# A transformer block on one core: where the biases of the projection are added, and on which engines its parts run

## The chip, the cores and the metric

The kernel runs on one core of a Trainium2 chip. The metric is the device time of one execution in microseconds (us); the time before is 3327.92 us, the median of 3 runs (3326.01 to 3333.78). One further execution was taken by the hardware profiler, and the rows below are from that one.

The core has five engines that run their own instruction lists and meet at semaphores: PE multiplies matrices and writes to PSUM, DVE and ACT and POOL work element by element, SP issues transfers.

## The reference

Four sequences of 1024 rows with 576 channels pass a block whose shifts, scales and gates come from a condition vector, and then a small rotation. What matters here:

```python
ada = silu(c) @ W_ada + b_ada
shift_msa, scale_msa, gate_msa, shift_mlp, scale_mlp, gate_mlp = split(ada, 6)
h = layernorm(x) * (1 + scale_msa) + shift_msa
x = x + gate_msa * (softmax_attention(h) @ W_proj + b_proj)
h = layernorm(x) * (1 + scale_mlp) + shift_mlp
x = x + gate_mlp * (gelu(h @ W_fc1 + b_fc1) @ W_fc2 + b_fc2)
x = rotate(x)
```

All of it is float32. A product of two float32 matrices is made of three products of rounded parts: each matrix is split into a high part (rounded) and a low part (what is left), and high x high, low x high and high x low are summed in PSUM. This is why there are so many instructions that make low parts.

## The kernel before

Six stages run one after another: preparation (ada, and the rotation matrices), the q, k, v products, attention, projection, feed-forward, rotation. A stage ends with a meeting of all engines.

**Preparation** also stores, beside the six parts of ada, two products: gate_msa x b_proj (GB_PROJ) and gate_mlp x b_fc2 (GB_FC2). So each bias can be added behind its gate.

**Attention** goes through 64 heads. SP loads each head's q, k, v three heads ahead (`load`), and sends the row maxima, which POOL has split, to the tiles that PE multiplies (`put_max`, L702). PE works through its list in order: the scores of a head cannot begin before its maxima have landed.

**Projection** works on 8 groups of 512 rows, in four subtiles t of 128 rows, and five channel tiles c of 128 (the last has 64). For a group g:
- *operand c*: PE spreads the reciprocal sums to 128 rows (`spread`, L1246), DVE multiplies the attention output with them (`operand`, L1105, tile p_of), ACT makes the high part (`operand_hi`, L1212), DVE the low part (`operand_lo`, L1110); both stand in p_oh.
- *product t*: PE multiplies p_oh with the weights p_w (`project`, L1258), 14 matmuls for each half of 288 columns, once all five operands of the group are there. DVE multiplies the result by the gate (`gate`, L1121) and adds the input rows (`residual`, L1126), to which POOL has added GB_PROJ (`biased_x`, L1059). The sum is p_x2.
- *statistics*: DVE's mean and variance (L1141 to L1158); then POOL normalises p_x2 into p_xn (L1071) and afterwards adds GB_FC2 to p_x2 (L1077), which SP stores for the next stage (L1017).
- *turn c*: PE transposes p_xn (L1285), ACT scales and shifts the result into the high part p_ht (L1232), DVE does the same in full precision into p_hf (L1191), POOL makes the low part (L1083), SP stores both (L1026).

The groups are interleaved by an order written out by hand, which every engine follows in its list. In the round of group g:

```python
ORDER = (("product", 0), ("product", 1), ("operand", 0), ("product", 2), ("operand", 1), ("turn", 0),
         ("turn", 1), ("product", 3), ("operand", 2), ("turn", 2), ("operand", 3), ("turn", 3),
         ("operand", 4), ("turn", 4))
```

Here "product" is of group g+1, "operand" of group g+2 and "turn" of group g. The statistics of group g come first in the round.

## Time and profile before

| what | us |
|---|---|
| median of 3 runs | 3327.92 |
| profiled execution | 3319.47 |
| its span | 3317.8 |
| attention's first and last matmul start | 727.16 and 1919.21 |
| projection's first product and last low part | 1948.12 and 2211.88 |
| feed-forward's first matmul | 2230.84 |
| PE, DVE, ACT, POOL busy over the span | 2939.1, 1698.6, 1400.5, 1525.1 |

An engine's busy time is summed over instructions that compute; issuing a transfer doesn't count. Matmuls overlap in the pipeline, so a row that merges 28 of them gives the time from the first start to the last end. In brackets stands the idle time of the engine before the row, and what ended it.

### The profile page before, as it was taken

To read this page: it belongs to the slowest core of one execution; us is meant where nothing else is said; L and a number is where in the kernel's file an instruction comes from. 1 tells how busy PE (TensorE), PEld (TensorE's weight loads), DVE (VectorE), ACT (ScalarE), POOL (GpSimd) and SP (SyncE) were. 2 spreads that over 40 slices of the span, in tenths; PEclk is the share of its full clock that TensorE was granted. 3 is DMA by queue.
4 is the path that set the end of the run, shared out by engine and by line. 5 is a ranking of instruction groups with operands and counts; after the bars stand their busy time and mean duration, and the time that the engine had idled before them with its cause. 6 is when DMAs were issued, how large, how long until landed. Compare 5 with 4: busy or idle time off the path is not lost. (4 is left out here: it accounts for less than half of the span.)

```text
span 3317.8 us, 49285 instructions
## 1 busy us (share of the span) xinstructions
PE 2939.1 (89%) x16066; PEld 2386.0 (72%) x16066; DVE 1698.6 (51%) x2862; ACT 1400.5 (42%) x1758; POOL 1525.1 (46%) x1143
## 2 busy tenths in 40 slices
PE   6759899968999999999999966849999999999976
PEld 2248777745666666666666645739999999999975
DVE  3446566546887888788887758741111111111125
ACT  2122222216888888888888822211111111111112
POOL 1232222115888878888888848752222222222210
PEclk9769899978999999999999978869999999999988
DMA  5365565552333333333333245658111121121144
GB/s 179 122 234 201 188 217 203 201 150 48 78 68 81 70 76 79 67 80 71 74 80 67 52 161 206 244 201 263 35 54 49 35 69 35 37 67 35 49 141 140
DMA packets 351132, 373.72 MB, mean 113 GB/s; under 512 B 179985, under 2 KB 243097, under 8 KB 350990
## 3 DMA queue, kind: packets, MB, share of 16 engines
q1 hardware_dynamic: 343512, 359.12, 36.4%
q10 hardware_dynamic: 7482, 12.69, 1.3%
q8 instruction: 95, 1.56, 0.2%
q14 instruction: 43, 0.35, 0.0%
HBM read 221.81 MB, written 149.36 MB: 112 GB/s over the span
## 5 line engine op out<-in xcount | busy, mean ns | idle before, releaser
L752 POOL TENSOR_TENSOR a_pl<-a_pf,a_ph 128x1024 fp32r<-128x1024 f32 x384 | 913.4, 2398 | 73.3 <-ACT a_pf L823 73.3
L769 DVE TENSOR_REDUCE a_mx<-a_psum_s 128x1 f32<-128x1024 f32 x512 | 625.9, 1222 | 246.4 <-PE a_psum_s L838 246.4
L821 ACT ACTIVATE a_ph<-a_psum_t 128x1024 fp32r<-128x1024 f32 x512 | 525.8, 1027 | 195.3 <-PE a_psum_t L853 195.0
L1407 POOL TENSOR_TENSOR m_al<-m_af,m_ah 128x256 fp32r<-128x256 f32 x288 | 212.1, 737 | 764.6 <-DVE m_ah L1416 764.6
L1455 PE MATMUL m_psum_h<-m_ht,m_w 128*128 128x256 f32 x4032 | 533.9, 284 | 31.7 <-DMA m_w<-w_s 23.0
L1455 PEld LDWEIGHTS m_psum_h<-m_ht,m_w 128*128 128x128 f32 x4032 | 508.5, 189 | 35.1 <-issue 34.0
L1416 DVE CAST m_ah<-m_af 128x256 fp32r<-128x256 f32 x288 | 84.6, 294 | 836.2 <-ACT m_af L1393 836.2
L1469 PE MATMUL m_psum_y<-m_w,m_ah 128*128 128x288 f32 x2304 | 505.2, 296 | 1.4 <-DVE m_y L1433 1.2
L1393 ACT ACTIVATE m_af<-m_psum_h,m_bias 128x256 f32<-128x256 f32 x288 | 137.0, 476 | 813.7 <-PE m_psum_h L1455 813.7
L838 PE MATMUL a_psum_s<-a_ks,a_qs 108*128 108x512 f32 x1024 | 425.0, 497 | 35.0 <-DVE a_mx L769 19.9
L838 PEld LDWEIGHTS a_psum_s<-a_ks,a_qs 108*128 108x128 f32 x1024 | 286.5, 327 | 197.9 <-DVE a_mx L769 171.3
L870 PE MATMUL a_psum_o<-a_ph,a_vs 128*100 128x512 f32 x1024 | 405.0, 395 | 3.7 <-POOL a_pl L752 3.6
L871 PE MATMUL a_psum_o<-a_pl,a_vs 128*100 128x512 f32 x1024 | 404.4, 395 | 0.0
L823 ACT ACTIVATE a_pf<-a_psum_t 128x1024 f32<-128x1024 f32 x384 | 391.8, 1020 | 0.0
L1469 PEld LDWEIGHTS m_psum_y<-m_w,m_ah 128*128 128x128 f32 x2304 | 384.5, 188 | 3.2 <-DVE m_y L1433 2.7
L853 PE MATMUL a_psum_t<-a_qs,a_ks 110*128 110x512 f32 x1024 | 335.1, 408 | 39.2 <-DVE a_pl L774 37.8
L1469 PE MATMUL m_psum_y<-m_w,m_al 128*128 128x288 f32 x1152 | 339.3, 295 | 0.0
L853 PEld LDWEIGHTS a_psum_t<-a_qs,a_ks 110*128 110x128 f32 x1024 | 187.5, 193 | 99.6 <-DVE a_pl L774 78.8
L584 PE MATMUL q_psum_pqk<-q_ht,q_w 128*128 128x512 f32 x1008 | 253.7, 410 | 0.0
L584 PEld LDWEIGHTS q_psum_pqk<-q_ht,q_w 128*128 128x128 f32 x1008 | 195.7, 197 | 48.7 <-issue 4.3
L871 PEld LDWEIGHTS a_psum_o<-a_pl,a_vs 128*100 128x100 f32 x1024 | 169.8, 166 | 67.9
L1469 PEld LDWEIGHTS m_psum_y<-m_w,m_al 128*128 128x128 f32 x1152 | 216.7, 188 | 0.0
(213 smaller groups left out, 3158.1 us busy)
## 6 DMA issues: line engine op xcount, KB each, us to landing
a_qs<-q_s SPq DMA_DIRECT2D x192, 144.0 KB
a_ks<-k_s SPq DMA_DIRECT2D x192, 144.0 KB
w_s<-q_ws SPq DMA_DIRECT2D x64, 324.0 KB, 3.4
h_s<-p_ht SPq DMA_DIRECT2D x40, 512.0 KB, 5.1
m_ht<-h_s SPq DMA_DIRECT2D x16, 1280.0 KB, 8.2
v_s<-q_vo SPq DMA_DIRECT2D x64, 288.0 KB, 2.3
a_vs<-v_s SPq DMA_DIRECT2D x128, 144.0 KB
q_s<-q_qko SPq DMA_DIRECT2D x32, 512.0 KB, 2.7
```

Of the source, the lines that this page charges most:

```text
L584: i = pe.matmul(pqk[:, m % 3], w[:, k, m * P:(m + 1) * P], ht[:, half, a, :], start=(n == 0), stop=(n == len(PASSES) - 1))
L752: pool.tensor_tensor(pl[:, s % RING], pf[:, s % RING], raw(ph[:, s % RING]), ALU.subtract).then_inc(lo_pool, 1)
L769: dve.tensor_reduce(mx[:, u % 2, t:t + 1], p_s[:], AX.X, ALU.max).then_inc(s_free, 1)
L821: act.activation(ph[:, s % RING], p_t[:, s % 2], ACT.Exp, scale=SCALE)
L823: act.activation(full, p_t[:, s % 2], ACT.Exp, scale=SCALE).then_inc(exp_done, 1)
L838: m = pe.matmul(p_s[:, h * 512:(h + 1) * 512], qs[0:SROWS, u, t:L:KT], ks[0:SROWS, u, h * 512:(h + 1) * 512], start=True, stop=True)
L853: m = pe.matmul(p_t[:, s % 2, r * GT:(r + 1) * GT], ks[0:MROWS, u, t * P:(t + 1) * P], qs[0:MROWS, u, lh * GT:(lh + 1) * GT], start=True, ...
L870: pe.matmul(p_o[0:VW, lh], vs[:, u, t], ph[:, s % RING, cols], start=(t == 0), stop=False)
L871: m = pe.matmul(p_o[0:VW, lh], vs[:, u, t], pl[:, s % RING, cols], start=False, stop=(t == KT - 1))
L1407: pool.tensor_tensor(al[:, f % RING], af[:, f % RING], raw(ah[:, f % RING]), ALU.subtract).then_inc(lo_ready, 1)
L1455: m = pe.matmul(p_h[:, f % RING, 0:GM], w1[:, k, f * P:(f + 1) * P], ht[:, q, a], start=(i == 0), stop=(i == len(PASSES) - 1))
L1469: m = pe.matmul(p_y[:, t, a, 0:HALF], part[:, f % RING, t * P:(t + 1) * P], w2[:, s, f, a * HALF:(a + 1) * HALF], start=(f == 0 and i == 0 ...
```

## The change

1. The bias b_proj enters the product itself. The weight tile gets one more slot, whose first 64 rows are the last channel tile's weights and whose next two rows are the bias (high and low part); the operand's last low tile, of which 64 rows are used, has ones in the other 64. The number of matmuls stays. GB_PROJ, its loads and POOL's `biased_x` go.
2. The second bias is written to x2_s ahead: at the start of attention, SP issues four transfers that copy the row GB_FC2 of each sequence to its 1024 rows (2.36 MB each). In projection, POOL issues a store that adds p_x2 to what stands there, in place of POOL's sum and SP's store.
3. The normalising moves from POOL to ACT, and the full-precision copy p_hf from DVE to ACT: ACT now makes p_ht and p_hf one after the other.
4. The operand's low part moves from DVE to POOL.
5. p_x2 is free for the next gate when SP, at the end of its round, has seen the store land (`x2b_done`). `operand` on DVE waits for POOL's low part of the group before (`ol_ready`), since p_of has one buffer.

Three places in the order of the engines' lists. On SP, at the start of attention (a_mh are the split maxima, x_s is x2_s):

```order
 L702 DMA a_qs<-a_mh 1x128x8 [waits a_mh_lo]
 L702 DMA a_qs<-a_mh 1x128x8
+L712 DMA x_s<-ada 1024x576 x4
 L674 UNCONDITIONAL_BRANCH
 L674 ISA
```

The four transfers stand between the maxima of head 0 and the loop, whose first transfer is the maxima of head 1.

On DVE, from the residual of product 3 to the statistics of the next round; before:

```order
L1126 TENSOR_TENSOR p_x<-p_x,p_xt 128x576 [waits p_gated]
L1104 REGISTER_ALU
L1105 TENSOR_TENSOR p_of<-p_ot,p_psum_r 128x512 [waits p_r_ready]
L1110 TENSOR_TENSOR p_oh<-p_of,p_oh 128x512 [waits p_oh_ready]
L1188 REGISTER_ALU
L1191 TENSOR_SCALAR p_hf<-p_psum_t,p_md 128x512 [waits p_lo_ready,p_hi_ready]
...
L1110 TENSOR_TENSOR p_oh<-p_of,p_oh 128x512 [waits p_oh_ready]
L957 REGISTER_ALU
L957 COMPARE_AND_BRANCH
L1141 BN_STATS p_stats<-p_x 128x6 [waits p_x2_ready]
```

and after (L1132 is the residual, L1116 the operand, L1147 the statistics):

```order
L1132 TENSOR_TENSOR p_x<-p_x,p_xt 128x576 [waits p_gated]
L1113 REGISTER_ALU
L1116 TENSOR_TENSOR p_of<-p_ot,p_psum_r 128x512 [waits p_ol_ready,p_r_ready]
...
L970 REGISTER_ALU
L970 COMPARE_AND_BRANCH
L1147 BN_STATS p_stats<-p_x 128x6 [waits p_x2_ready]
```

The low parts of the operand and the full copies are gone from between the operands, and each operand waits for one semaphore more.

On POOL, from the last low part of one round through the next; before:

```order
L1083 TENSOR_TENSOR p_ht<-p_hf,p_ht 128x512 [waits p_full_ready]
L1067 ISA
L1071 TENSOR_SCALAR p_xn<-p_x,p_rstd,p_shift 128x576 [waits p_t_ready,p_rstd_ready]
L1071 TENSOR_SCALAR p_xn<-p_x,p_rstd,p_shift 128x64
...
L1077 TENSOR_TENSOR p_x<-p_x,p_gt 128x576 [waits p_xn_ready]
...
L1083 TENSOR_TENSOR p_ht<-p_hf,p_ht 128x512 [waits p_full_ready]
...
L1059 TENSOR_TENSOR p_xt<-p_xt,p_gt 128x576 [waits p_x_in1]
```

and after (L1083 is the adding store, L1073 the operand's low part, L1090 that of h):

```order
L1090 TENSOR_TENSOR p_ht<-p_hf,p_ht 128x512 [waits p_full_ready]
L1083 ISA [waits p_x2_ready]
L1083 DMA x_s<-p_x 128x4x576
L1072 ISA
L1073 TENSOR_TENSOR p_oh<-p_of,p_oh 128x512 [waits p_oh_ready]
...
L1089 ISA
L1090 TENSOR_TENSOR p_ht<-p_hf,p_ht 128x512 [waits p_full_ready]
```

Normalising and both bias sums are gone; the store and five low parts of the operand have come, the latter between those of h as the written order has them.

The diff, cut to its core:

```diff
                     load(hd, hd)
                 put_max(0, 0)
+                for b in range(B):
+                    sp.dma_start(x2_s[b * L:(b + 1) * L],
+                                 ada[b:b + 1, GB_FC2 * C:(GB_FC2 + 1) * C].broadcast_to([L, C])).then_inc(bias_out, 16)
...
+    BIAS = W_TILES
+    LOW_REM = A_TILES - 1
+    passes = PASSES[:-1] + [(LOW_REM, BIAS)]
...
-        w = sb("w", [P, W_TILES, C], F32R)
+        w = sb("w", [P, W_TILES + 1, C], F32R)
+        bf = sb("bf", [1, C])
+        bs = sb("bs", [1, 2, C], F32R)
...
                 def load_x(g, b, half):
                     sp.dma_start(xt[:, half], x[bass.ds(g * GT, GT), :].rearrange("(t p) c -> p t c", p=P)) \
                       .then_inc(x_in[half], 16)
-                    for i, s in enumerate((GATE_MSA, GB_PROJ)):
-                        sp.dma_start(gt[:, half, i], ada[bass.ds(b, 1), s * C:(s + 1) * C].broadcast_to([P, C])) \
-                          .then_inc(x_in[half], 16)
+                    sp.dma_start(gt[:, half], ada[bass.ds(b, 1), GATE_MSA * C:(GATE_MSA + 1) * C]
+                                 .broadcast_to([P, C])).then_inc(x_in[half], 16)
 
                 def load_mod(b, half):
-                    sp.dma_start(gt[:, half, 2], ada[bass.ds(b, 1), GB_FC2 * C:(GB_FC2 + 1) * C].broadcast_to([P, C])) \
-                      .then_inc(md_in[half], 16)
                     sp.dma_start(md[:, half], mod[bass.ds(b, 1)].rearrange("a p n -> (a p) n")) \
                       .then_inc(md_in[half], 16)
...
                 load_o(0, 0, 0)
+                sp.dma_start(bf[:], b_proj.rearrange("(a n) -> a n", a=1)).then_inc(b_in, 16)
                 load_x(0, 0, 0)
                 sp.wait_ge(rs_made, 1)
                 sp.dma_start(rsums.rearrange(flat, n=NHEAD * L // P), rs_flat[:]).then_inc(rs_out, 16)
                 sp.wait_ge(rs_out, 16)
                 load_rs(0, 0)
                 load_split_weight(sp, w, wproj, slice(0, C), w_in)
+                sp.dma_start(raw(w[0:REM, BIAS]), wproj[0, FULL * P:C]).then_inc(w_in, 16)
+                sp.wait_ge(set_up, 5)
+                sp.wait_ge(bias_lo, 1)
+                sp.dma_start(raw(w[REM:REM + 2, BIAS]), raw(bs[:])).then_inc(bias_in, 16)
                 load_mod(0, 0)
...
                         load_x(g + 2, b + 1, half)
-                    sp.wait_ge(x2b_ready, g + 1)
-                    sp.dma_start(x2_s[bass.ds(g * GT, GT), :].rearrange("(t p) c -> p t c", p=P), x2[:, half]) \
-                      .then_inc(x2b_out[half], 16)
...
                           .then_inc(h_out[c], 16)
                     if more >= 2:
                         load_mod(b + 1, half)
-
+                    wait_alone(sp, x2b_out[half], 16 * (b + 1), x2b_done[half])
...
-                def biased_x(g, b, half):
-
-                    pool.wait_ge(x_in[half], 48 * (b + 1))
-                    for t in range(SUB):
-                        i = pool.tensor_tensor(xt[:, half, t], xt[:, half, t], gt[:, half, 1], ALU.add)
-                    i.then_inc(xb_ready, 1)
-
-                biased_x(0, 0, 0)
-                biased_x(1, 0, 1)
+                pool.memset(raw(w[REM:P, BIAS]), 0.0).then_inc(set_up, 1)
+                pool.wait_ge(set_up, 4)
+                pool.memset(raw(oh[REM:P, :, LOW_REM]), 1.0).then_inc(set_up, 1)
+                pool.wait_ge(set_up, 5)
+
+                def operand_lo(g, half, c):
+                    r = P if c < FULL else REM
+                    pool.wait_ge(oh_ready, NK * g + c + 1)
+                    pool.tensor_tensor(oh[0:r, half, NK + c], of[0:r, c], raw(oh[0:r, half, c]), ALU.subtract) \
+                        .then_inc(ol_ready, 1)
+
+                for g in range(2):
+                    for c in range(NK):
+                        operand_lo(g, g, c)
 
                 def body(g, b, half, more):
-                    if not (isinstance(g, int) and g == 0):
-                        pool.wait_ge(t_ready, START + NK * g)
-                    wait_alone(pool, rstd_ready, g + 1, passed)
-                    for t in range(SUB):
-                        for a, z, o in ((0, C, 0), (FULL * P, C, C)):
-                            i = pool.tensor_scalar(xn[:, t, o:o + z - a], x2[:, half, t, a:z],
-                                                   rstd[:, t:t + 1], shift[:, t:t + 1], ALU.mult, ALU.add)
-                    i.then_inc(xn_ready, 1)
-                    pool.wait_ge(md_in[half], 32 * (b + 1))
-                    pool.wait_ge(xn_ready, START + g + 1)
-                    for t in range(SUB):
-                        i = pool.tensor_tensor(x2[:, half, t], x2[:, half, t], gt[:, half, 2], ALU.add)
-                    i.then_inc(x2b_ready, 1)
-                    for c in range(NK):
-                        if c == 2 and more == 2:
-                            biased_x(g + 2, b + 1, half)
-                        pool.wait_ge(full_ready, NK * g + c + 3)
-                        pool.tensor_tensor(ht[:, NK + c], hf[:, c_slot(half, c)], raw(ht[:, c]), ALU.subtract) \
-                            .then_inc(lo_ready, 1)
+
+                    pool.wait_ge(x2_ready, g + 1)
+                    pool.dma_start(x2_s[bass.ds(g * GT, GT), :].rearrange("(t p) c -> p t c", p=P), x2[:, half],
+                                   accum_op=ALU.add).then_inc(x2b_out[half], 16)
+                    for what, n in ORDER:
+                        if what == "operand" and more == 2:
+                            operand_lo(g + 2, half, n)
+                        if what == "turn":
+                            pool.wait_ge(full_ready, NK * g + n + 3)
+                            pool.tensor_tensor(ht[:, NK + n], hf[:, c_slot(half, n)], raw(ht[:, n]), ALU.subtract) \
+                                .then_inc(lo_ready, 1)
...
-                dve.tensor_copy(sel[:, 0:C], heads[:]).then_inc(set_up, 1)
-                dve.tensor_copy(sel[:, C:CPAD], heads[:, FULL * P:C]).then_inc(set_up, 1)
+                dve.tensor_copy(sel[:, 0:C], heads[:]).then_inc(sel_made, 1)
+                dve.tensor_copy(sel[:, C:CPAD], heads[:, FULL * P:C]).then_inc(sel_made, 1)
+                dve.wait_ge(bias_hi, 1)
+                dve.tensor_tensor(bs[:, 1], bf[:], raw(bs[:, 0]), ALU.subtract).then_inc(bias_lo, 1)
 
...
                 def operand(g, half, c):
 
                     dve.wait_ge(r_ready, NK * g + c + 1)
+                    if not (isinstance(g, int) and g == 0):
+                        dve.wait_ge(ol_ready, NK * (g - 1) + c + 1)
                     dve.tensor_tensor(of[:, c], ot[:, c], p_r[:, c_slot(half, c)], ALU.mult) \
                        .then_inc(of_ready, 1)
 
-                def operand_lo(g, half, c):
-                    dve.wait_ge(oh_ready, NK * g + c + 1)
-                    dve.tensor_tensor(oh[:, half, NK + c], of[:, c], raw(oh[:, half, c]), ALU.subtract) \
-                       .then_inc(ol_ready, 1)
-
                 def gate(g, b, half, t, a):
 
                     if t == 0 and a == 0:
-                        dve.wait_ge(xb_ready, g + 1)
+                        dve.wait_ge(x_in[half], 32 * (b + 1))
                         if not (isinstance(g, int) and g < 2):
-                            dve.wait_ge(x2b_out[half], START + 16 * b)
+                            dve.wait_ge(x2b_done[half], START + b)
                     dve.wait_ge(p_ready, 2 * (SUB * g + t) + a + 1)
                     cols = slice(a * HALF, (a + 1) * HALF)
-                    dve.tensor_tensor(x2[:, half, t, cols], p_p[:, t % 2, a, 0:HALF], gt[:, half, 0, cols],
+                    dve.tensor_tensor(x2[:, half, t, cols], p_p[:, t % 2, a, 0:HALF], gt[:, half, cols],
                                       ALU.mult).then_inc(gated, 1)
...
                         if what == "operand" and more == 2:
                             operand(g + 2, half, n)
-                            if n:
-                                operand_lo(g + 2, half, n - 1)
-                        if what == "turn":
-                            dve.wait_ge(hi_ready, NK * g + n + 1)
-                            dve.wait_ge(lo_ready, NK * g + n + 1)
-                            k = 2 * NK + n
-                            dve.tensor_scalar(hf[:, c_slot(half, n)], p_t[:, c_slot(half, n)],
-                                              md[:, half, k + NK:k + NK + 1], md[:, half, k:k + 1],
-                                              ALU.mult, ALU.add).then_inc(full_ready, 1)
-                    if more == 2:
-                        operand_lo(g + 2, half, NK - 1)
...
+                act.wait_ge(b_in, 16)
+                act.activation(bs[:, 0], bf[:], ACT.Copy).then_inc(bias_hi, 1)
                 for g in range(2):
                     sums_hi(g, g)
                     for c in range(NK):
...
-                    act.wait_ge(md_in[half], 32 * (b + 1))
+                    act.wait_ge(t_ready, START + NK * g)
+                    wait_alone(act, rstd_ready, g + 1, passed)
+                    for t in range(SUB):
+                        for a, z, o in ((0, C, 0), (FULL * P, C, C)):
+                            i = act.activation(xn[:, t, o:o + z - a], x2[:, half, t, a:z], ACT.Identity,
+                                               bias=shift[:, t:t + 1], scale=rstd[:, t:t + 1])
+                    i.then_inc(xn_ready, 1)
+                    act.wait_ge(md_in[half], 16 * (b + 1))
                     for what, n in ORDER:
                         if what == "operand" and more == 2:
                             operand_hi(g + 2, half, n)
...
                             act.wait_ge(h_out[n], START + 16 * g)
                             act.wait_ge(t_ready, START + NK * g + n + 1)
                             k = 2 * NK + n
-                            act.activation(ht[:, n], p_t[:, c_slot(half, n)], ACT.Identity,
-                                           bias=md[:, half, k:k + 1], scale=md[:, half, k + NK:k + NK + 1]) \
-                               .then_inc(hi_ready, 1)
+                            act.wait_ge(lo_ready, NK * g + n + 1)
+                            for dst in (ht[:, n], hf[:, c_slot(half, n)]):
+                                i = act.activation(dst, p_t[:, c_slot(half, n)], ACT.Identity,
+                                                   bias=md[:, half, k:k + 1], scale=md[:, half, k + NK:k + NK + 1])
+                            i.then_inc(full_ready, 1)
...
-                        for n, (k, j) in enumerate(PASSES):
+                        for n, (k, j) in enumerate(passes):
                             i = pe.matmul(p_p[:, t % 2, a, 0:HALF], oh[:, half, k, t * P:(t + 1) * P],
                                           w[:, j, a * HALF:(a + 1) * HALF],
-                                          start=(n == 0), stop=(n == len(PASSES) - 1))
+                                          start=(n == 0), stop=(n == len(passes) - 1))
...
-                pe.wait_ge(set_up, 5)
+                pe.wait_ge(sel_made, 2)
                 for c in range(NK):
                     spread(0, 0, c)
-                pe.wait_ge(w_in, 64)
+                pe.wait_ge(w_in, 80)
+                pe.wait_ge(bias_in, 16)
...
-                pool.wait_ge(b_in, 32)
-                for i, g in enumerate((GATE_MSA, GATE_MLP)):
-                    pool.tensor_tensor(av[:, (SEC + i) * C:(SEC + i + 1) * C], av[:, g * C:(g + 1) * C], bb[:, i],
-                                       ALU.mult).then_inc(bias_gated, 1)
+                pool.wait_ge(b_in, 16)
+                pool.tensor_tensor(av[:, GB_FC2 * C:(GB_FC2 + 1) * C], av[:, GATE_MLP * C:(GATE_MLP + 1) * C], bb[:],
+                                   ALU.mult).then_inc(bias_gated, 1)
```

## Rows read from the trace of the kernel before

**Rows 1.** One projection round: us; PE, PEld, DVE, ACT, POOL busy; clock, DMA, GB/s.

```profile
2039.00:2071.50 32.50, 23.25 (x142) 20.07 (x142) 26.94 (x49) 7.29 (x12) 26.66 (x22) 0.82 0.65 227
```

**Rows 2.** Timeline of PE: start us, us, operation, [idle before <-releaser].

```profile
1975.16 10.27 PE L1258 MATMUL p_psum_p<-p_w,p_oh 128*128 128x288 f32 x56 [2.74 <-DVE p_oh L1110]
...
2039.53 8.97 PE L1258 MATMUL p_psum_p<-p_w,p_oh 128*128 128x288 f32 x56 [6.18 <-DVE p_oh L1110]
...
2054.50 3.95 PE L1258 MATMUL p_psum_p<-p_w,p_oh 128*128 128x288 f32 x28
...
2168.73 12.89 PE L1258 MATMUL p_psum_p<-p_w,p_oh 128*128 128x288 f32 x84 [6.09 <-issue]
```

**Rows 3.** Timeline of DVE, behind the last product of that round.

```profile
2058.90 0.81 DVE L1121 TENSOR_TENSOR p_x<-p_psum_p,p_gt 128x288 f32<-128x288 f32 x2
2059.75 1.73 DVE L1126 TENSOR_TENSOR p_x<-p_x,p_xt 128x576 f32<-128x576 f32 x1
2061.40 0.67 DVE L1105 TENSOR_TENSOR p_of<-p_ot,p_psum_r 128x512 f32<-128x512 f32 x1
...
2070.34 0.94 DVE L1110 TENSOR_TENSOR p_oh<-p_of,p_oh 128x512 fp32r<-128x512 f32 x1
```

**Rows 4.** Instructions by tile: duration ns min/median/max, first and last start us.

```profile
L1232 ACT ACTIVATE p_ht<-p_psum_t,p_md x40: 758/762/778, 1992.5 to 2210.2; 128x512 fp32r<-128x512 f32 x40
L1083 POOL TENSOR_TENSOR p_ht<-p_hf,p_ht x40: 1257/1273/1821, 1994.1 to 2211.9; 128x512 fp32r<-128x512 f32 x40
...
L1126 DVE TENSOR_TENSOR p_x<-p_x,p_xt x32: 757/1148/2064, 1955.1 to 2186.7; 128x576 f32<-128x576 f32 x32
...
L1212 ACT ACTIVATE p_oh<-p_of x40: 629/631/635, 1942.2 to 2165.2; 128x512 fp32r<-128x512 f32 x40
```

**Rows 5.** Table of DMA issues: queue, count, KB each, median us to landing.

```profile
p_xt<-in_x_dram SPq DMA_DIRECT2D x8, 1152.0 KB, 7.5
x_s<-p_x SPq DMA_DIRECT2D x8, 1152.0 KB, 4.5
...
m_xt<-x_s SPq DMA_DIRECT2D x32, 288.0 KB, 3.9
...
a_qs<-a_mh SPq DMA_DIRECT2D x128, 4.0 KB, 2.0
```

**Rows 6.** Timelines of DVE and of PE at the stage's start.

```profile
1941.44 0.69 DVE L1105 TENSOR_TENSOR p_of<-p_ot,p_psum_r 128x512 f32<-128x512 f32 x1 [1.37 <-PE p_psum_r L1246]
...
1948.12 17.57 PE L1258 MATMUL p_psum_p<-p_w,p_oh 128*128 128x288 f32 x112 [2.60 <-DVE p_oh L1110]
```

**Rows 7.** Timelines of PE, DVE and POOL at the stage's end.

```profile
2182.26 3.95 PE L1258 MATMUL p_psum_p<-p_w,p_oh 128*128 128x288 f32 x28
...
2201.20 1.97 PE L1285 MATMUL p_psum_t<-p_ident,p_xn 128*128 128x128 f32 x8 [11.91 <-POOL p_xn L1071]
...
2191.04 2.97 DVE L1141 BATCH_NORM_STATS2 p_stats<-p_x 128x6 f32<-128x288 f32 x8
...
2196.43 4.71 POOL L1071 TENSOR_SCALAR p_xn<-p_x,p_rstd,p_shift 128x576 f32<-128x576 f32 x8 [3.78 <-issue]
...
2211.88 1.26 POOL L1083 TENSOR_TENSOR p_ht<-p_hf,p_ht 128x512 fp32r<-128x512 f32 x1 [0.22 <-DVE p_hf L1191]
```

**Rows 8.** Timelines of SP's queue and of PE at attention's start.

```profile
748.28 25.45 SPq L702 DMA_DIRECT2D a_qs<-a_mh  x4
...
785.33 0.64 PE L853 MATMUL a_psum_t<-a_qs,a_ks 110*128 110x512 f32 x2
```

**Rows 9.** Tables of stretches: an idle one, and the one with most bytes.

```profile
750.00:760.00 10.00, 4.98 (x8) 2.21 (x8) 4.65 (x5) 0.00 (x0) 0.00 (x0) 0.50 0.01 0
...
2250.00:2300.00 50.00, 48.44 (x376) 47.26 (x375) 4.41 (x15) 6.99 (x15) 10.82 (x15) 1.00 0.96 310
```

**Rows 10.** Tile p_gt: its broadcast loads from ada.

```profile
DMA to landing us min/median/max: 4.3/7.9/9.0
```

**Rows 11.** Timeline of POOL in preparation: the two bias products.

```profile
144.29 2.74 POOL L1795 TENSOR_TENSOR c_av<-c_av,c_bb 4x576 f32<-4x576 f32 x2 [29.63 <-ACT c_av L1849]
```

47 lines of the change are left out of this document (22 added, 25 removed).

## The prediction

> **What bounds the kernel now.** The profiled execution took 3319.47 us. The change touches three stages: preparation, attention, and above all projection, which stands between the last attention matmul at 1919 us and the feed-forward stage at 2218 us. I read, in this order: the table of stretches for one projection round, the timeline of PE and of DVE through that round, the durations by tile, the timelines at the end and the beginning of the stage, and last the start of attention, because the change puts four large transfers there.
>
> A steady round of projection is 32.5 us long, and in it PE works 23.3 us, DVE 26.9 and POOL 26.7, ACT 7.3 [rows 1]. No engine is full; the round is a circle of waits. PE starts the products of a group at 2039.53 and ends them at 2058.45 (2054.50 plus 3.95): 18.92 us, its transposes and spreads included. It had been idle for 6.18 us before, waiting for p_oh from DVE [rows 2]. The first of these starts is at 1975.16, the last at 2168.73; six rounds lie between, so the period is 193.57 / 6 = 32.26 us [rows 2]. What fills the 13.3 us after PE's last product is DVE alone: gate at 2058.90, residual sum, then operand, low part, full copy in turn, until the last low part of the operand ends at 2071.28 [rows 3]. PE starts after it. So what DVE does between a group's last product and its last low part is the price of a round, and the work of POOL and ACT shows only where DVE waits for it or is slowed by it.
>
> **The loop.** The change takes the five low parts of the operand (L1110) and the five full copies (L1191) from DVE. DVE keeps gate, residual and operand, and the low parts go to POOL, which loses the normalising, the two bias sums and gets the issue of a transfer. ACT gets the normalising and the full copies. The circle after it, from PE's first product: 18.92 us to the last product; half a gate, 0.45; the residual; one operand, 0.67 [rows 3]; the high part on ACT, 0.63; then POOL, in order, low part 2 of the operand, low part 2 of h, operand 3, h 3, operand 4: five instructions of L1083's shape at a median of 1.27 us, 6.35 in all [rows 4]; and some 0.6, an estimate, for the five hand-overs between engines. ACT feeds POOL fast enough: per tile it does one high part and two copies, 0.63 + 2 x 0.76 = 2.15 us, against POOL's 2.54 [rows 4]. The residual had 1.73 us in that place [rows 3], but its shortest is 0.76 and its median 1.15 [rows 4]; POOL is less busy there now, so I take 1.15. The sum is 28.8 us, 3.5 less than 32.26, and over six rounds 20.8 us. Bounds: with the residual at 0.76 the round is 28.4 us and the gain 23; with every low part at its longest, 1.82, and the residual at 2.06, it is 32.4 and nothing is gained.
>
> Under this cover other things cost nothing. DVE does its statistics while POOL is still in its chain, so the 5 us that DVE stood before the next gates are gone from its path; ACT's eight normalising instructions end some 6 us after PE's start, and PE wants the first of them after 14. DVE's gate now waits until SP has passed the stores of the round before and seen the accumulating store land: SP gets there some 2.5 us after PE's start, and PE wants the gate after 9. The transfers of a round are 0.6 MB fewer (two broadcast rows).
>
> **The accumulating store.** No row shows a transfer issued by POOL, nor one that adds. Its plain form lands in 4.5 us [rows 5]. An adding one reads its target too; three passes at that price are 13.5 us. It may take 30, a round and the first gate's slack, before the gate of the group after next is late, so I count 0. The issue itself occupies POOL, where nothing else stands between the last low part of a round and the first of the next, some 9 us, and about 15 pass before the chain at the round's end is pushed. From 0 to 15 us of issue the cost is 0; beyond that it is rival 2.
>
> **Start and end of the stage.** At the start the low parts of groups 0 and 1 stand in a row on POOL instead of between DVE's operands. Group 0: operand at 1941.44, 0.69, high part 0.63, five low parts 6.35, so PE starts at 1949.3 and not at 1948.12 [rows 6]; twice that is 2.4 us lost (1 to 5). The bias tile comes with two more transfers behind the weights, 147 KB and 5 KB, and two fills on POOL. Before, PE waited for p_oh there and not for weights [rows 6], and now it waits 1.2 us longer: I count 0, and 1 us if the last of them lands later.
>
> At the end the last statistics start on DVE at 2191.04, after five full copies; without these they start right after the last residual, at about 2187.5, since the last product ends at 2186.21: 3.5 us. The normalising takes 4.71 us on POOL; on ACT, from 0.76 us per 512 columns, four times about 0.86 and four short ones, some 4.4: 0.3. Then POOL adds the second bias ahead of its first low part, and from PE's first transpose at 2201.20 to the last low part's end at 2213.14 there are 11.9 us; with two copies per tile on ACT (five times 1.45), the first transposes and one low part it is 9.7: 2.2 us [rows 7]. Together 6.0 gained (3 to 7).
>
> **Attention.** Four transfers of 2.36 MB, 9.4 MB in all from one row of ada to x2_s, are issued on SP's queue after the first maxima (748.28) and ahead of the second pair, which SP issues at the end of that row, near 773 [rows 8]. The transfer engines are idle then (busy share 0.01) [rows 9]. The second pair is wanted by PE at 785.33, where the scores of head 1 begin [rows 8]; what is queued behind is PE itself, in order, so with it the values of head 0 and everything after. The head-3 load stands there too, but is wanted only some 10 us later. The fill's speed decides. Fastest row: 310 GB/s [rows 9], 30.4 us, ended at 780, nothing lost. Slowest: a broadcast of the same ada row lands in 4.3 us at best for 288 KB [rows 10], and 2.0 of these a 4 KB transfer takes too [rows 5], so 128 GB/s, 74 us, 40 lost. Nearest: whole rows of 2304 bytes, 1152 KB in 7.5 us and 288 KB in 3.9 [rows 5], so 3.6 us per 0.885 MB: 38.4 us from 749.5, and 2 for the maxima to land, 790: 5 us lost. I take 5.
>
> The Trainium skill (DMA: Bandwidth & Descriptors, section Latency and other measured facts) gives 207 to 214 GB/s for copies from HBM to HBM. No row here shows such a copy; by its figure, an estimate, the fill would take 45 us, the loss would be about 12 and not 5, and the sum would be -12.4 us, 3315.5.
>
> In preparation POOL loses one of two products, 1.4 us [rows 11]; PE reads what POOL makes after them only behind the series for the rotation, which DVE and PE are still at. I count 0; with that cover gone it would be 1.4 gained.
>
> **Sum.** -20.8 + 2.4 - 6.0 + 5 = -19.4 us, on 3319.47 us: 3300.1. The median of the runs shown, 3327.92, is 8.5 us above the profiled one; nothing of the change depends on that, so I forecast 3308.5.
>
> **Rivals.**
> 1. The fill holds the queue much longer (the other side). At the broadcast row's rate it costs 40 us where I count 5: 3308.5 + 35 = 3343.5, slower. For: the row of ada is read 4096 times, and everything SP issues after goes through the same queue. Against: the 4.3 us hold the latency of one small transfer. It decides from about 145 GB/s down, where the loss passes 31 us.
> 2. POOL becomes the bound. It issues a transfer in the loop that SP issued before, and its low parts are now all of the circle's tail. If the issue takes over 20 us of POOL, or the low parts stretch to 1.8 us beside DVE, the round stays at 32 us: the gain is the end of the stage alone, -6.0 + 2.4 + 5, about +1: 3329. For: L1083 has a longest of 1.82. Against: the DVE instructions left beside the chain are statistics and operands, which read one SBUF tile each, and the long L1083 stood beside the two-tile low parts that leave DVE.
> 3. The fill is wholly hidden and the residual sum undisturbed: -23 + 1 - 7 = -29, 3299.
>
> **How the numbers follow.** What cannot be told from no change is 0.2%, 6.7 us: faster means below 3321.3, slower above 3334.6. The forecast, with up to 12 us more or 8 less than its sum, has 0.65, and its own range is 3300 to 3320; rival 3 has 0.08; rival 2 has 0.14, of which nearly all is no change; rival 1 has 0.13, of which 0.11 is slower. So faster 0.74, same 0.14, slower 0.12. The range leaves out the worst half of rival 1 and the best of rival 3: 3297 to 3332.
>
> **What would show it.** Right: PE's product starts 28.4 to 29.6 us apart; each p_oh wait of PE put down to POOL, some 4.5 us; DVE's statistics starting before PE's next products; the stretch from the first product of the stage (1948.12) to the last low part of h (2213.14), 265 us before, shorter by some 25; PE waiting a few us for the maxima of head 1 near 785. Wrong: a round of 32 us with POOL busy throughout (rival 2), a gap on PE of tens of us near 785 (rival 1), or ACT's normalising ending later than PE's first transposes, which would make ACT the new wait.

## The result and the profile after

The changed kernel takes 3339.09 us (median of 8 runs, 3335.49 to 3342.32), the kernel before 3327.35 beside it (8 runs): a ratio of 1.0032, 95% interval 1.0021 to 1.0043. It is slower by some 11 us, where 3308.5 us and faster was forecast. One place makes the difference, and it is not in the projection stage.

**Attention.** First the timeline of SP's queue in the changed kernel (start, us, operation), where [rows 8] had the two pairs of maxima in one row:

```profile
753.60 30.52 SPq L712 DMA_DIRECT2D x_s<-ada  x4
784.35 19.49 SPq L702 DMA_DIRECT2D a_qs<-a_mh  x2
```

The four transfers that fill x2_s are issued from 753.60 on and hold SP for 30.5 us. The maxima of head 1 are issued only behind them, at 784.35, and their issue takes another 19.5 us. PE's timeline around the scores of head 1, which started at 785.33 before [rows 8]:

```profile
788.86 0.65 PE L842 MATMUL a_psum_s<-a_ks,a_qs 108*128 108x512 f32 x2
826.90 1.21 PE L857 MATMUL a_psum_t<-a_qs,a_ks 110*128 110x512 f32 x2 [37.39 <-DMA a_qs<-a_mh]
```

PE stands still for 37.39 us and waits for these maxima. The table of stretches (columns as in [rows 1]) says what the transfer engines did meanwhile:

```profile
755.00:765.00 10.00, 4.73 (x9) 2.05 (x8) 4.90 (x4) 0.00 (x0) 0.00 (x0) 0.50 0.90 132
775.00:785.00 10.00, 8.13 (x27) 5.72 (x27) 3.73 (x4) 8.16 (x9) 8.37 (x6) 0.75 1.03 136
815.00:825.00 10.00, 0.00 (x0) 0.00 (x0) 0.00 (x0) 0.00 (x0) 0.00 (x0) 0.50 1.01 158
```

They are full (share 0.90 to 1.03), at 132 to 158 GB/s in these rows; until 785, with almost nothing but the fill to move, 132 to 136. In [rows 9] they idled at 755, and a full stretch moved 310 GB/s. 9.44 MB at 135 GB/s take 70 us, so the fill lasts to about 824.

**Projection.** PE's timeline, the starts of product series and the first matmul of the feed-forward stage:

```profile
1991.84 16.58 PE L1261 MATMUL p_psum_p<-p_w,p_oh 128*128 128x288 f32 x112 [3.75 <-POOL p_oh L1073]
...
2018.99 9.23 PE L1261 MATMUL p_psum_p<-p_w,p_oh 128*128 128x288 f32 x56 [4.03 <-POOL p_oh L1073]
...
2077.59 8.97 PE L1261 MATMUL p_psum_p<-p_w,p_oh 128*128 128x288 f32 x56 [4.63 <-POOL p_oh L1073]
...
2092.57 3.95 PE L1261 MATMUL p_psum_p<-p_w,p_oh 128*128 128x288 f32 x28
...
2106.20 9.92 PE L1261 MATMUL p_psum_p<-p_w,p_oh 128*128 128x288 f32 x56 [4.11 <-POOL p_oh L1073]
...
2194.48 13.83 PE L1261 MATMUL p_psum_p<-p_w,p_oh 128*128 128x288 f32 x84 [4.17 <-issue]
...
2251.73 4.84 PE L1459 MATMUL m_psum_h<-m_ht,m_w 128*128 128x256 f32 x28 [20.07 <-DMA m_w<-w_s]
```

The six steady rounds last (2194.48 - 2018.99) / 6 = 29.25 us, against 32.26 [rows 2]. The wait in front of each of the six is put down to POOL, 4.0 to 4.6 us. One round in the table of stretches:

```profile
2077.59:2106.20 28.61, 23.23 (x142) 20.08 (x143) 17.91 (x40) 14.92 (x25) 13.71 (x12) 0.86 0.76 230
```

POOL's busy time is 13.7 us instead of 26.7 and DVE's 17.9 instead of 26.9 [rows 1]. Behind the last product, DVE no longer sets PE's start. Its timeline, and then POOL's, in the same round:

```profile
2097.05 1.28 DVE L1132 TENSOR_TENSOR p_x<-p_x,p_xt 128x576 f32<-128x576 f32 x1
2098.25 1.27 DVE L1116 TENSOR_TENSOR p_of<-p_ot,p_psum_r 128x512 f32<-128x512 f32 x2
2099.83 0.69 DVE L1116 TENSOR_TENSOR p_of<-p_ot,p_psum_r 128x512 f32<-128x512 f32 x1 [0.31 <-PE p_psum_r L1249]
2100.44 2.97 DVE L1147 BATCH_NORM_STATS2 p_stats<-p_x 128x6 f32<-128x288 f32 x8
```

```profile
2099.67 1.27 POOL L1073 TENSOR_TENSOR p_oh<-p_of,p_oh 128x512 fp32r<-128x512 f32 x1 [1.96 <-ACT p_oh L1204]
2101.00 1.27 POOL L1090 TENSOR_TENSOR p_ht<-p_hf,p_ht 128x512 fp32r<-128x512 f32 x1
2102.23 1.27 POOL L1073 TENSOR_TENSOR p_oh<-p_of,p_oh 128x512 fp32r<-128x512 f32 x1
2103.45 1.27 POOL L1090 TENSOR_TENSOR p_ht<-p_hf,p_ht 128x512 fp32r<-128x512 f32 x1
2104.68 1.25 POOL L1073 TENSOR_TENSOR p_oh<-p_of,p_oh 64x512 fp32r<-64x512 f32 x1
...
2107.11 1.26 POOL L1083 DMA_DIRECT2D x_s<-p_x  x1
```

DVE is done with operand 4 at 2100.5 and goes on to the statistics before PE's next products. POOL works through five low parts in a row, 1.23 us from one to the next, and PE starts when the fifth ends, at 2106.2 (2104.68 plus 1.25, and 0.3 on the way). The issue of the store costs POOL 1.26 us. At the end of the stage (timelines of DVE, ACT and POOL):

```profile
2214.22 2.98 DVE L1147 BATCH_NORM_STATS2 p_stats<-p_x 128x6 f32<-128x288 f32 x8
...
2220.33 4.46 ACT L1222 ACTIVATE p_xn<-p_x,p_shift,p_rstd 128x576 f32<-128x576 f32 x8 [2.11 <-DVE p_shift L1164]
...
2233.48 1.26 POOL L1090 TENSOR_TENSOR p_ht<-p_hf,p_ht 128x512 fp32r<-128x512 f32 x1 [0.31 <-ACT p_hf L1235]
```

The last statistics stand 1.33 us behind the last product (2212.89) instead of 4.83 [rows 7]; the normalising takes 4.46 us on ACT; the last low part ends at 2234.74. From the stage's first product that is 242.9 us instead of 265.0. The adding store lands 12.8 us after its issue, and one of the four fill transfers 45.6, both at the median (table of DMA issues: count, KB each, median us to landing):

```profile
x_s<-ada SPq DMA_DIRECT2D x4, 2304.0 KB, 45.6
...
x_s<-p_x POOLq DMA_DIRECT2D x8, 1152.0 KB, 12.8
```

**The two profiled executions**, 3317.8 and 3338.9 us of span, term by term (differences of the starts above and of [rows 2], [rows 6] and [rows 8]):

```
                                        forecast   measured
preparation (to the scores of head 0)      0         +4.1
the gap at head 1, and attention after    +5        +37.5, +1.0
start of the stage, two groups            +2.4       +1.3
six rounds                               -20.8      -18.1
from the last round's start on            -6.0       -4.9
feed-forward and after                     0         +0.2
sum                                      -19.4      +21.1
```

The 4.1 us of preparation are no cost of the change. One matmul of attention, which PE starts behind ACT's first exponentials of head 0, starts at 769.80 before and 773.87 after, but at 770.73 to 775.64 in the first four kernels below and at 769.16 in u1, which share the changed kernel's preparation word for word. The granted clock differs there: between 100 and 130 us it was 0.89 in the profile of before, 0.72 in that of after. The profile of before is also one of its shorter executions, 8 us under the median; so the medians differ by 11.7 us and not by 21.1.

### The profile page after: what moved, and what is told of

It is laid out like the page before. It is cut to its first block and busy times, and to the rows that moved or that the text cites. A ratio compares the mean times of both kernels' runs of the same rounds, so it can differ in the third digit from the quotient of the medians.

```text
span 3338.9 us, 49234 instructions
## 1 busy us (share of the span) xinstructions
PE 2944.9 (88%) x16066; PEld 2384.9 (71%) x16066; DVE 1632.0 (49%) x2783; ACT 1462.5 (44%) x1863; POOL 1432.1 (43%) x1064
## 3 DMA queue, kind: packets, MB, share of 16 engines
q0 software_dynamic: 4224, 9.44, 1.6%
```

## The experiments

**Is it the fill, and how could it be hidden?** In e1 it is cut into 64 pieces, one per head:

```diff
-                for b in range(B):
-                    sp.dma_start(x2_s[b * L:(b + 1) * L], ada[b:b + 1, ...].broadcast_to([L, C]))
 ...
                     for lh in range(LH):
                         store(hd, lh)
+                    rows = L * SLOTS // NHEAD
+                    sp.dma_start(x2_s[bass.ds(u * L + rows * i, rows)], ada[u:u + 1, ...].broadcast_to([rows, C]))
```

> The fill is cut into 64 pieces of 64 rows, one at the end of SP's work for each head. Theory A (the 37.4 us gap of PE at head 1 is the fill standing in SP's queue ahead of the second maxima, and is the whole of the loss): the gap at 789 goes, no other appears, and the median falls by 36 to 38 us from 3339 to about 3302, some 25 us under the kernel before. Theory B (9.4 MB more of transfers in attention cost their time wherever they stand): the 64 pieces cost about 1 us each, attention ends as late as before the cut, median 3335 to 3345. Theory C (part of the loss is in preparation, 4 us, and after the gap, 1 us): preparation still ends 4 us later than in the kernel before, median about 3306.

Measured: 3301.69 us (6 runs) against 3325.60 of before beside it, ratio 0.9929 (0.9916 to 0.9941). PE's timeline:

```profile
789.22 0.73 PE L858 MATMUL a_psum_t<-a_qs,a_ks 110*128 110x512 f32 x2 [0.26 <-DVE a_pl L779]
...
1982.79 9.50 PE L1262 MATMUL p_psum_p<-p_w,p_oh 128*128 128x288 f32 x56 [4.31 <-POOL p_oh L1074]
...
2158.89 13.82 PE L1262 MATMUL p_psum_p<-p_w,p_oh 128*128 128x288 f32 x84 [4.17 <-issue]
```

The gap is gone (0.26 us), rounds last (2158.89 - 1982.79) / 6 = 29.35 us, as with the fill in one go (29.25). Theory A holds. The raw medians fall by 37.4 us (3339.09 to 3301.69), the very length of the gap, but that exactness is chance: against the kernel before that ran beside each, the change lost 11.7 us and e1 gains 23.9, so some 36 us lie between them, uncertain by some 5. Within that the gap is the whole loss. Theory C falls: head 0 comes at 775.64 here, later still than in the changed kernel, and the time fell all the same. Without the gap the change gains 23.9 us; the forecast's terms without the fill sum to 24.4, which is in part luck too, since the six rounds gave 17.5 here and not 20.8.

**Is it the order in SP's queue?** e2 issues the same four transfers at the same time on POOL's queue.

```diff
-                    sp.dma_start(x2_s[b * L:(b + 1) * L], ...)   # SP, behind the first maxima
+                    pool.dma_start(x2_s[b * L:(b + 1) * L], ...) # POOL, behind its split of the first maxima
```

> The same four transfers at the same time, but issued by POOL on its own queue; SP's queue holds only the maxima and loads behind them. If the order in SP's queue is what costs: the maxima of head 1 land within 3 to 6 us, the gap at 789 is under 6 us, median about 3302 to 3307. If the busy transfer engines are what costs (they serve the fill first whatever the queue): the gap stays 25 us or more, median 3328 to 3340. A third outcome: POOL's issue of four times 1024 rows takes so long that its low parts of head 0 start late, which would show as PE waiting for POOL near 770.

Measured: 3330.45 us, ratio 1.0014 (1.0005 to 1.0024). PE's timeline has two gaps now:

```profile
794.44 1.22 PE L857 MATMUL a_psum_t<-a_qs,a_ks 110*128 110x512 f32 x2 [7.96 <-DMA a_qs<-a_mh]
...
823.75 1.24 PE L842 MATMUL a_psum_s<-a_ks,a_qs 108*128 108x512 f32 x2 [19.46 <-DMA a_vs<-v_s]
```

8.0 us for the maxima, 19.5 for the values of a later head: 27.4 together, so 10 of the 37.4 were the order in the queue. The rest is paid on POOL's queue too, while the transfer engines are full (share 0.97 to 1.01 until 775, at 131 to 136 GB/s). POOL's issue took 3.3 us for all four, and PE did not wait for POOL. Both single theories fall short; the second comes nearer.

**Why 135 GB/s?** e3, e5 and e6 keep the transfers on SP's queue, but copy rows of x, each read once; e4 writes a row that was loaded to SBUF, the core's own memory. The source in each, and in e5 and e6 the target in the same order:

```diff
-    ada[b:b + 1, GB_FC2 * C:(GB_FC2 + 1) * C].broadcast_to([L, C])
+    x[b * L:(b + 1) * L]                                             # e3
+    x[b * L:(b + 1) * L].rearrange("(a t) c -> t a c", t=2)          # e5; e6 with t=16
+    fb[:]   # e4, 32 stores of 128 rows; fb is loaded once from ada
```

> The four transfers copy 4096 different rows of x instead of one row of ada per batch (the second bias is replaced by these rows, so the output is another one). If reading one row over and over is what holds the fill at 132 to 137 GB/s: the copies run above 200 GB/s, end within 46 us, the gap at 789 shrinks from 37 to under 15 us. If memory to memory with rows of this size is the limit: the same 132 to 137 GB/s and a gap of 35 to 40 us.

> The row of batch 0 is loaded once to 128 partitions (4 to 5 us) and written 32 times from there (all batches get the bias of batch 0, so the output is another one). If the write to memory in rows of 2304 bytes is the limit: 132 to 137 GB/s again, the gap at 789 stays 35 us or more, plus the 4 us of the load. If the read side is: 200 GB/s or more, some 45 us with the load, gap under 20 us.

> The four transfers copy 4096 different rows of x again, but even rows first and then odd ones, so that no two rows lie together and each piece is 2304 bytes, as in the changed kernel (the second bias is replaced by these rows, so the output is another one). If reading one row over and over holds the fill at 135 GB/s: 280 GB/s or more, as with whole rows together (325 GB/s between 755 and 775), and no gap at 789. If it was the larger pieces that made the copy of different rows fast: 135 to 180 GB/s and a gap of 20 us or more.

> 4096 different rows of x again in pieces of one row, but every 16th row after another, so that 16 series are there to share out (with two series only two of the 16 transfer engines worked, 52 GB/s together, 26 each; the second bias is replaced by these rows, so the output is another one). If reading one row over and over holds the fill at 135 GB/s, 8.4 for each engine: now 280 GB/s or more, 18 or more for each engine, and no gap of PE at head 1. If pieces of 2304 bytes from memory to memory are the limit with all engines at work: 135 to 180 GB/s and a gap of 20 us or more.

The table of stretches in e3 (3304.32 us), e4 (3298.88), e5 (3457.72) and e6 (3297.62, each one run), a stretch in which the transfers run; the last two columns are the share of the transfer engines and GB/s:

```profile
765.00:775.00 10.00, 5.54 (x11) 3.08 (x11) 4.27 (x4) 2.09 (x3) 0.07 (x1) 0.50 1.04 324
```

```profile
765.00:775.00 10.00, 5.41 (x10) 2.93 (x10) 3.90 (x4) 4.05 (x5) 2.04 (x1) 0.50 1.01 387
```

```profile
805.00:825.00 20.00, 0.00 (x0) 0.00 (x0) 0.00 (x0) 0.00 (x0) 0.00 (x0) 0.50 0.13 52
```

```profile
765.00:775.00 10.00, 5.64 (x11) 3.16 (x12) 3.67 (x3) 5.37 (x6) 2.70 (x3) 0.50 1.00 315
```

324, 387, 52 and 315 GB/s. In e3 the pieces had also become larger: between 755 and 775, 6.49 MB went in 308 packets. So e5 was to bring back pieces of one row, and went astray: with an outer dimension of two the share was 0.13, about two of the 16 engines, PE waited 150.57 us at head 1, and the time rose to 3458. e6 gives 16 series to share out: all engines work, 6.35 MB go in 2792 packets of about a row each between 755 and 775, at 315 to 317 GB/s, and as in e3 and e4 no gap is left at head 1. So pieces of 2304 bytes are not the limit, nor is the way from memory to memory, nor the write side (e4). In e2, too, the same row went in larger packets (3.99 MB in 883 of them between 755 and 785) and no faster, at 133 GB/s. What is left is the source: one row of ada, read 1024 times. One thing was not tried apart: e3, e5 and e6 read another tensor as well (x, an input, where ada is made by the kernel), so a copy of different rows of ada is missing. Why such a source is slow, no run here shows.

**Which part of the change shortens the rounds?** From here all kernels but d1 have e1's spread fill (u4 has none), and one part is undone in each. The results, with the starts on PE of the first steady series, of the last, and of feed-forward, and what follows from them:

```
kernel                        first    last     feed-fwd  round   last to feed-fwd
before                        1975.16  2168.73  2230.84   32.26   62.11
e1: change, fill spread       1982.79  2158.89  2215.06   29.35   56.17
u1: normalising on POOL       1976.28  2152.39  2207.82   29.35   55.43
u2: full copies on DVE        1980.96  2163.44  2222.25   30.41   58.81
u3: operand low parts on DVE  1977.37  2143.01  2198.11   27.61   55.10
u4: POOL adds second bias     1976.95  2152.82  2213.56   29.31   60.74
d1: before, copies on ACT     1975.75  2152.12  2212.90   29.40   60.78
v2: u3, ACT in other order    1974.54  2137.12  2193.12   27.10   56.00
```

u1 puts the eight normalising instructions back behind POOL's store:

```diff
-                            i = act.activation(xn[:, t, o:o + z - a], x2[:, half, t, a:z], ACT.Identity, ...)
+                            i = pool.tensor_scalar(xn[:, t, o:o + z - a], x2[:, half, t, a:z], ..., ALU.mult, ALU.add)
```

> The changed kernel with the fill in 64 pieces, and the normalising back on POOL. Theory A (the chain of POOL's low parts after the last product sets the round; the normalising lies beside PE's products on either engine): rounds of 29.0 to 29.6 us as with it on ACT, the stage's end 0 to 1 us later, median within 2 us of 3302. Theory B (POOL's relief is what shortened the round): rounds of 30.5 us or more, median 3310 or more.

3297.78 us, ratio 0.9921 (0.9903 to 0.9939), which can't be told from e1's. Rounds are the same to 0.01 us, the end 0.7 us earlier and not later. In the rounds the normalising was off the path on either engine; behind the last product PE waits for it on either, 4.71 us on POOL and 4.46 on ACT.

u2 puts the full copies back on DVE, in the order of before:

```diff
-                            for dst in (ht[:, n], hf[:, c_slot(half, n)]):   # both on ACT
+                            act.activation(ht[:, n], ...).then_inc(hi_ready, 1)
+                            # DVE, turn n: dve.tensor_scalar(hf[:, c_slot(half, n)], p_t[:, c_slot(half, n)], ...)
```

> The changed kernel with the fill in 64 pieces, and the full copies back on DVE. Theory A (POOL's five low parts, 6.2 us in a row, set the round; DVE's copies fit beside them): rounds of 29.0 to 30.0 us, the end of the stage 2 to 4 us later because the last statistics stand behind five copies, median 3303 to 3310. Theory B (the copies on DVE were what the round of before paid for): each of the three copies after the last product, 0.8 us, delays PE: rounds of 31.5 us or more, median 3316 or more.

3310.25 us, ratio 0.9950 (0.9933 to 0.9966): 1.06 us a round, and 2.6 at the end. It lies between the theories. DVE's and PE's timelines:

```profile
2099.34 0.68 DVE L1118 TENSOR_TENSOR p_of<-p_ot,p_psum_r 128x512 f32<-128x512 f32 x1
2101.38 0.81 DVE L1194 TENSOR_SCALAR p_hf<-p_psum_t,p_md 128x512 f32<-128x512 f32 x1 [1.36 <-ACT p_ht L1242]
...
1980.96 9.71 PE L1268 MATMUL p_psum_p<-p_w,p_oh 128*128 128x288 f32 x56 [3.81 <-POOL p_oh L1075]
...
2163.44 12.71 PE L1268 MATMUL p_psum_p<-p_w,p_oh 128*128 128x288 f32 x84 [4.75 <-issue]
```

Between its operands DVE waits 1.36 us for ACT's high part and then copies, so operand 4 comes later; POOL's chain hides a part of that. Not all of the 1.06 us is this wait: the first 56 products of a round take 10.19 us on average here and 9.74 in e1, so 0.45 us of it stands in PE's own work.

u3 puts the low parts of the operand back on DVE, each behind the next operand, as before the change:

```diff
-            pool.tensor_tensor(oh[0:r, half, NK + c], of[0:r, c], raw(oh[0:r, half, c]), ALU.subtract)
+            dve.tensor_tensor(oh[0:r, half, NK + c], of[0:r, c], raw(oh[0:r, half, c]), ALU.subtract)
```

> The changed kernel with the fill in 64 pieces, and the low parts of the operand back on DVE. Theory A (DVE had two kinds of work too much after the last product, and taking away either is enough): DVE does three operands and four low parts, 0.7 and 1.3 us each, after the last residual, and PE starts as early as behind POOL's chain: rounds of 28.5 to 29.8 us, the start of the stage 1 to 2 us earlier, median 3298 to 3305. Theory B (the low parts on DVE were what the round paid for): rounds of 31 us or more, median 3312 or more.

3289.91 us, ratio 0.9891 (0.9874 to 0.9908): better than theory A, and 1.7 us a round better than e1. Of these, 0.5 us are faster products (the first 56 take 9.25 us on average, 9.74 in e1), and some 1.2 us come from the shorter tail behind the last product. PE's timeline, and the low parts by tile (duration ns min/median/max):

```profile
1977.37 9.85 PE L1261 MATMUL p_psum_p<-p_w,p_oh 128*128 128x288 f32 x56 [2.73 <-DVE p_oh L1109]
...
2143.01 12.74 PE L1261 MATMUL p_psum_p<-p_w,p_oh 128*128 128x288 f32 x84 [2.68 <-issue]
```

```profile
L1109 DVE TENSOR_TENSOR p_oh<-p_of,p_oh x40: 677/684/1347, 1945.6 to 2141.6; 128x512 fp32r<-128x512 f32 x32, 64x512 fp32r<-64x512 f32 x8
```

The low part takes 0.68 us on DVE at the median, where it took 1.27 on POOL. Moving it was a loss: POOL's chain of five is longer than what DVE would have needed. The median hides two sizes. While POOL does nothing a low part takes 0.68 to 0.69 us (28 of 40); beside one of POOL's low parts of h it takes 1.34 to 1.35 (12 of 40). DVE's timeline in one round, then POOL's:

```profile
2110.94 0.68 DVE L1109 TENSOR_TENSOR p_oh<-p_of,p_oh 128x512 fp32r<-128x512 f32 x1
...
2112.37 1.35 DVE L1109 TENSOR_TENSOR p_oh<-p_of,p_oh 128x512 fp32r<-128x512 f32 x1 [0.15 <-ACT p_oh L1204]
```

```profile
2111.89 1.27 POOL L1079 TENSOR_TENSOR p_ht<-p_hf,p_ht 128x512 fp32r<-128x512 f32 x1 [3.29 <-ACT p_hf L1235]
```

u4 adds the second bias on POOL, as before, and stores plainly; there is no fill.

```diff
-                    pool.dma_start(x2_s[...], x2[:, half], accum_op=ALU.add)
+                    for t in range(SUB):   # once xn_ready
+                        i = pool.tensor_tensor(x2[:, half, t], x2[:, half, t], g2[:, half], ALU.add)
+                    pool.dma_start(x2_s[...], x2[:, half])
```

> The changed kernel without the fill; POOL adds the second bias from a broadcast row, as before the change, and stores x2 plainly on its own queue. Theory A (POOL has some 9 us free after a round's last low part, the four additions fit there): rounds of 29.0 to 29.8 us as with the adding store, the stage's end 1 to 4 us later, because the additions stand ahead of the last low parts, median 3302 to 3307. Theory B (the additions were part of what the round of before paid for): rounds of 30.5 us or more, median 3311 or more.

3306.05 us, ratio 0.9950 (0.9935 to 0.9965). Theory A: the rounds are the same. POOL's timeline at the stage's end shows the price, 4.6 us, a little over the 1 to 4 expected:

```profile
2182.98 5.48 POOL L1086 TENSOR_TENSOR p_x<-p_x,p_g 128x576 f32<-128x576 f32 x4 [5.55 <-ACT p_xn L1228]
2188.75 0.77 POOL L1089 DMA_DIRECT2D x_s<-p_x  x1 [0.30 <-POOL p_x L1086]
```

The additions (5.48 us) stand ahead of the last low parts. So the adding store gains 4.6 us, once, at the end of the stage.

d1 is the kernel before with one edit, both copies of a turn on ACT.

> The kernel before with one edit: the full copies on ACT. Theory A (this edit is nearly all of the projection stage's gain; POOL's 26.7 us of work still fit): rounds of 27.6 to 28.8 us against 32.3, the stage's end 3 to 5 us earlier, median 3292 to 3302. Theory B (POOL, with normalising, two bias sums and low parts, sets the round once DVE is relieved): rounds of 30 us or more, median 3307 or more.

3304.59 us, ratio 0.9949 (0.9934 to 0.9964): between the theories. This edit alone takes 17.7 us off, three quarters of what the change gains without its fill, but the rounds last 29.4 us, not the 27.6 of u3. PE's timeline, and DVE's low parts by tile:

```profile
1975.75 9.67 PE L1253 MATMUL p_psum_p<-p_w,p_oh 128*128 128x288 f32 x56 [2.73 <-DVE p_oh L1110]
...
2152.12 13.87 PE L1253 MATMUL p_psum_p<-p_w,p_oh 128*128 128x288 f32 x84 [3.59 <-issue]
```

```profile
L1110 DVE TENSOR_TENSOR p_oh<-p_of,p_oh x40: 682/1295/1881, 1944.7 to 2150.1; 128x512 fp32r<-128x512 f32 x40
```

PE still waits for DVE. With POOL at its old work (normalising, two bias sums, low parts) the same low part takes DVE 1.30 us at the median, with POOL relieved 0.68. The trace of d1 shows both within one kernel: 10 of the 40 low parts meet no work of POOL and take 0.68 to 0.69 us; the other 30 stand beside one of the bias sums and take 1.29 to 1.88, 24 of them beside `biased_x`. The change removes both sums. So POOL's work was on the path after all, not in its own time but in DVE's.

v2 is u3 with ACT's high parts of operands 3 and 4 ahead of its copies of turn 3:

```diff
+    COPY_ORDER = (..., ("operand", 2), ("turn", 2), ("operand", 3), ("operand", 4), ("turn", 3), ("turn", 4))
-                    for what, n in ORDER:        # ACT's loop
+                    for what, n in COPY_ORDER:
```

> The changed kernel with the fill in 64 pieces, the operand's low parts back on DVE (that was 27.6 us a round), and ACT's high part of operand 4 ahead of its two copies of turn 3 (in the round read, DVE's last low part started when ACT's last high part ended, which stood behind four copies). If ACT's order sets PE's start: rounds of 26.0 to 26.9 us, median 3278 to 3286. If DVE's own chain or PE's last turn does: rounds of 27.3 us or more, median 3288 or more.

3280.79 us, ratio 0.9884 (0.9868 to 0.9899): 1.2% under the kernel before, the lowest median of all. PE's timeline:

```profile
1974.54 9.68 PE L1264 MATMUL p_psum_p<-p_w,p_oh 128*128 128x288 f32 x56 [2.73 <-DVE p_oh L1112]
...
2137.12 13.94 PE L1264 MATMUL p_psum_p<-p_w,p_oh 128*128 128x288 f32 x84 [1.89 <-issue]
```

27.10 us a round is 0.5 less than u3, not 0.7 to 1.6; from the ratios to the kernel before, whose intervals overlap, the two can't be told apart. The wait in front of the products did shrink, from 2.7 to 3.4 us to 2.1 in five of the six steady rounds. One first series in v2, then in u3 (table of stretches; the third column from the right is the granted clock):

```profile
2055.55:2065.55 10.00, 10.00 (x56) 9.85 (x56) 6.91 (x24) 6.28 (x12) 3.47 (x3) 0.73 1.07 343
```

```profile
2061.01:2070.01 9.00, 9.00 (x57) 8.84 (x57) 6.77 (x24) 4.82 (x9) 2.26 (x2) 0.83 1.07 334
```

The 56 products take 10.0 us at a granted clock of 0.73 of full speed, against 9.0 at 0.83. Over the six rounds they take 10.0 us on average against 9.25, so 0.7 us of what the order gained is lost there. Whether the shorter wait is the cause was not tried; in the changed kernel, behind waits of 4.0 to 4.6 us, they took 9.0 to 10.5.

## Why the forecast was wrong

**The step that failed** is the speed of the fill. The prediction bounded it by three rows and took the nearest: "whole rows of 2304 bytes, 1152 KB in 7.5 us and 288 KB in 3.9", 38.4 us and a loss of 5. Nearest meant the size of a piece. What decided was the source: a row read over and over, and of that kind there was one row, the broadcast load of ada [rows 10], the slow end of the range. It gave 128 GB/s, 74 us and a loss of 40; measured were 132 to 136 GB/s, 70 us and 37.4. This was rival 1, "from about 145 GB/s down", with a time of 3343.5; 3339.1 came. The argument against it, that the 4.3 us hold a small transfer's latency, had already been met by taking 2.0 off, so it counted twice, and the rival's 0.13 was too little. The slow end was a measurement of the same kind of source, not a mishap. The prediction also saw the price in the order of SP's queue alone; by e2, 27.4 of the 37.4 us are paid on POOL's queue as well.

The Trainium skill (DMA: Bandwidth & Descriptors, section Latency and other measured facts) has 207 and 214 GB/s for copies of tiles of 128 rows of 16 KiB between HBM tensors, at a row pitch of 512 KiB and at one padded by 4 KiB. No run here copies such tiles, and the figure fits none of the copies that were run: 315 to 324 with different rows, 132 to 136 with one row, 52 with two engines.

**The loop** was right in mechanism: 28.4 to 29.6 us forecast, 29.25 measured, PE waiting for POOL as said (4.4 us on average, 4.5 forecast). The gain of 18.1 instead of 20.8 comes from the product term. The 18.92 us from first to last product were read in one round; over the six rounds of the changed kernel they are 18.93 to 20.39, 19.6 on average, because the first 56 products take 9.0 to 10.5 us. In the kernel before the average is 19.7 as well: its mean period was set against the products of its fastest round. That cost 4.0 us over six rounds. The tail behind the last product was 9.66 us (29.25 - 19.59), 9.88 forecast, and gave 1.3 back, though the residual in it took 1.28 (taken: 1.15).

**What the forecast did not ask:** whether moving the low parts is a gain at all. It counted the move as a relief of DVE and priced POOL's chain rightly, but not DVE's low part with POOL relieved, 0.68 us at the median (u3) and not the 1.30 beside POOL's old work (d1). The row for the residual, 0.76 alone and up to 2.06 beside POOL [rows 4], held the hint.

**Smaller terms.** Start of the stage: +1.3 (2.4, within 1 to 5). End: -4.9 (-6.0): the statistics gained their 3.5 us and the low parts 2.05 of 2.2; but the products of the last round took 0.9 longer and the small DVE operations between statistics and normalising 0.7; from the last low part to feed-forward it was 0.7 less. The adding store landed in 12.8 us (13.5) and its issue took 1.26, so both cost nothing in the loop, as said; that it makes three passes, no run shows. Rival 2 did not come about.

## What to carry to other kernels

Price a transfer by the row whose source is like it, even if that row looks like the worst case, and ask of every bulk transfer which small one stands behind it and who waits for that; cut into pieces behind each head's work, the same bytes left no gap here. When an engine is relieved, ask again what its neighbour's instructions now take, before moving those too: DVE's low part was slow where it met POOL's sums, and moving it to POOL as well cost 12 us (e1 against u3), some 3 of them in slower products. A period averaged over rounds must be set against parts averaged over the same rounds.

## What the runs showed of the hardware

Reading one 2304-byte row of ada 1024 times per transfer ran at 132 to 136 GB/s with all transfer engines full; 4096 different rows of x in the same pieces ran at 315, a row from SBUF at 387. A transfer whose outer dimension is 2 kept about two of 16 engines busy (share 0.13, 52 GB/s, e5), one of 16 all of them (share 1.00, e6). A small transfer on another queue than the fill's still came some 20 us late (e2: split by 773.5, PE at 794.4). The subtraction of two 128x512 tiles took DVE 0.68 to 0.69 us while POOL did nothing, 1.34 to 1.35 beside POOL's own two-tile subtractions (u3), and 1.29 to 1.88 beside its two-tile sums (d1).
